# A graph network on one core: edge tiles counted in items of mixed width, and strays gathered by tile

## Chip, cores and metric

One core of one Trainium2 chip. The metric is the device time of one launch in microseconds. A profiled execution of the same kernel gives the trace from which the rows below are read.

## What is computed

6250 nodes with 128 features and 100,000 edges (src, dst), sorted by dst; dst is 6250 u^2 for a uniform u, so the first target nodes have by far the most edges. The layer normalized and rectified x goes through two SAGE convolutions, then through an edge network with batch norm:

```python
def _sage_conv(x, src, dst, W_nbr, W_root, b):
    msgs = x[src]
    summed = jax.ops.segment_sum(msgs, dst, num_segments=N)
    deg = jax.ops.segment_sum(jnp.ones((src.shape[0], 1), x.dtype), dst, num_segments=N)
    agg = summed / jnp.maximum(deg, 1.0)
    return agg @ W_nbr + x @ W_root + b

z = jnp.concatenate([h[src], h[dst], edge_attr], axis=1) @ W.T + b
z = (z - mean) * jax.lax.rsqrt(var + BN_EPS) * gamma + beta
msg = jax.nn.sigmoid(z[:, :H]) * jax.nn.softplus(z[:, H:])
out = x + h + jnp.zeros_like(h).at[src].add(msg)
```

## The kernel before, in words

The nodes are padded to 49 windows of 128 (NT = 49), the edges to 784 tiles of 128, four tiles to a group, 196 groups (NG). The stages follow each other: layer norm, convolution 0, its node products, sort tables, convolution 1, node products and the p and q tables, the edge pass (pass 1, with a gather from p_tab per tile), the message pass (pass 2, with a scatter per tile), the sum of the sorted rows, the output.

**The two convolutions** sum messages x[src] by dst in two ways.

*Counted tiles*: the first 304 tiles (DT), where dst spans few nodes. For a tile, DVE makes two one-hots (`tile_low`: src within its window, 128 wide; `tile_hot`: source window and target slot, up to 392 wide; L1322 to L1331), PE multiplies them (L1667, L1671) into a count matrix of source node by target slot, and ACT copies it to SBUF as bf16 (L918, L922). A unit has eight slots; the first 128 tiles are taken in pairs of two times four slots. Sixteen units are an item, 15 items in all. The item's counts are multiplied with the features of all 49 windows (`final`, L1677, 49 matmuls with 384 columns, the features in three bf16 parts, plus a degree column in convolution 0). The result, 128 target slots by 128 features, goes through ACT and DVE and is added to the sums by window (`sum_acc`, L1697). The counts are stored to DRAM in convolution 0 and loaded again by ACT in convolution 1, so the tiles are built once. An *extra* loop at half way (`conv_extra`) repeats an item's tiles for targets beyond the eighth slot; its least number of rounds is one.

*Gathered groups*: the other 120 groups (76 to 195). POOL gathers the source rows of each tile by indirect DMA (`gather_all`, L826), four to a group, into a ring of eight groups (RP). DVE makes a one-hot of dst against a window (`sum_by_window`, L1221), PE multiplies rows and one-hot (L1687, and the degree column in L1691), DVE adds the sum (L1211). The matmul in L1756 marks a group done, and POOL may then refill its place.

**The order** is written by hand in `conv_slot` of each engine and run by `in_conv`: part 0 has END = 4 slots, part 1 has 7 turns of 2 x CS = 16 slots, part 2 has 4 slots. A slot is one gathered group and a share of the item work (`BUILT`, `FINAL`): in part 0 the first item is built and the features are split into bf16 parts by ACT and DVE in turn (L905, L910, L1338, L1346); in a turn two items are built while the two before them are multiplied. In the first 14 slots of a turn stands one *sort job* each (a histogram by source window in convolution 0, a rank in convolution 1: L1743, L1748, L1749 on PE, L1229, L1236, L1239 on DVE), in every second of these one *root job* (x @ W_root + b for one window: turned by L1727, multiplied by L1731, bias added by L1732, in convolution 1 also x by L1735; copied by ACT, L945). A rank needs a row of `base_tab`, which SP loads when the rank before is done (L689), with x for the root jobs (L697) and the zeroing of rows of m_tab (L669) in the same queue.

POOL waits between groups only for the place in the ring (L821 to L822):

```python
if g >= first + depth:
    pool.wait_ge(freed, before + g - first - depth + 1)
```

## Time and profile before

| | us |
|---|---|
| median of 3 runs | 3615.26 (3613.3 to 3619.41) |
| the profiled execution, own time | 3627.41 |
| its span | 3625.6 |
| busy PE, DVE, ACT, POOL | 2500.5, 1878.3, 1409.1, 2499.9 |
| POOL gathers of the two convolutions (L826 from h_tab) | 956, 958.0 busy |
| mean granted TensorE clock | 0.834 of full |

The profiled execution is one run with its own time; shares and rows are of its span. A busy engine is not yet one that sets the end: what ended an engine's idle time, and whose, says more. The granted clock is 0.5 or 1.0 at any moment (1.2 or 2.4 GHz) and its mean stands in the stage rows.

### The profile page before, as it was taken

The numbers are of one execution on the slowest core, as the hardware profiler recorded it, in microseconds if no ns is written. First come the engines' busy times: TensorE is split into PE (matmuls) and PEld (weight loads), VectorE is DVE, ScalarE is ACT, GpSimd is POOL, SyncE is SP. The second block draws the span as 40 slices with busy tenths as digits, with TensorE's granted clock in tenths as the row PEclk, the third lists the DMA queues.
The fourth block names the chain that finished last, engine by engine and source line by source line (L and its number), as shares of the span: only waits on it lengthen the run. The fifth ranks groups of instructions, "written<-read, shape, count | busy, mean of one in ns | idle before, by whom it ended". The sixth has DMA issues, their size and how long they took to land.

```text
span 3625.6 us, 63849 instructions
## 1 busy us (share of the span) xinstructions
PE 2500.5 (69%) x14630; PEld 1714.2 (47%) x14631; DVE 1878.3 (52%) x4147; ACT 1409.1 (39%) x2642; POOL 2499.9 (69%) x2536
## 2 busy tenths in 40 slices
PE   1888888678888897888888898982222223666348
PEld 0656666545555565544444444441111113656248
DVE  6755655455566665533333333355434335878448
ACT  4333322120100004422222222229878787878600
POOL 5777777477777760777777777765777777777730
PEclk9889988878899998999999999995555556988579
DMA  4444444345455632798888888885544445887358
GB/s 123 150 135 133 133 167 142 121 150 182 155 188 188 203 105 76 256 297 289 290 290 285 288 290 287 290 267 188 175 158 145 159 153 206 292 294 276 113 191 264
DMA packets 337734, 733.52 MB, mean 202 GB/s; under 512 B 66489, under 2 KB 130333, under 8 KB 333761
## 3 DMA queue, kind: packets, MB, share of 16 engines
q1 hardware_dynamic: 242289, 489.81, 38.6%
q0 software_dynamic: 93152, 218.16, 20.1%
q10 hardware_dynamic: 2160, 24.09, 1.7%
q8 instruction: 45, 0.74, 0.1%
q14 instruction: 88, 0.72, 0.1%
HBM read 456.75 MB, written 275.07 MB: 202 GB/s over the span
## 4 chain that ended last, share of the span: by engine, by line
POOL 39%; PE 24%; issue 16%; DMA 6%; DVE 6%; ACT 6%; DVEq 2%; SPq 0%; ACTq 0%; POOLq 0%
POOL m_tab L855 16%; POOL arena L826 8%; POOL H L826 8%; POOL Q L826 7%; PE PS L1687 6%; PE PS L1677 5%; PE PS L1873 3%; DMA m_tab<-Q,pos_i 3%; PE PS L1749 2%; PE PS L1852 1%; PE PS L1857 1%; DMA Q<-base_tab 1%; ACT H L871 1%; DMA H<-p_tab,src_i 1%; PE PS L1843 1%
## 5 line engine op out<-in xcount | busy, mean ns | idle before, releaser
L826 POOL DMA_INDIRECT Q<-h_tab,src_i x956 | 958.0, 1002 | 334.2 <-issue 285.9
L855 POOL DMA_INDIRECT m_tab<-Q,pos_i x782 | 776.5, 993 | 260.2 <-issue 229.2
L1882 PE MATMUL PS<-ident,arena 128*128 128x128 f32 x784 | 193.5, 394 | 621.2 <-DVE arena L1567 377.0
L1687 PE MATMUL PS<-Q 128*128 x2668 | 430.6, 309 | 175.2 <-DVE arena L1211 93.3
L826 POOL DMA_INDIRECT H<-p_tab,src_i x398 | 381.0, 957 | 221.9 <-issue 119.7
L1057 ACT ACTIVATE arena<-PS,LB 128x512 f32<-128x512 f32 x392 | 248.0, 684 | 715.7 <-PE PS L1857 702.2
L1687 PEld LDWEIGHTS PS<-Q 128*128 128x128 f32 x2668 | 366.7, 212 | 260.9 <-issue 257.3
L1882 PEld LDWEIGHTS PS<-ident,arena 128*128 128x128 f32 x784 | 125.8, 197 | 682.8 <-issue 345.1
L826 POOL DMA_INDIRECT arena<-p_tab,src_i x384 | 365.5, 952 | 117.0 <-issue 114.9
L1857 PE MATMUL PS<-arena,WC 128*128 128x512 f32 x784 | 369.4, 593 | 0.0
L1852 PE MATMUL PS<-H,Q 128*128 x1464 | 358.1, 387 | 0.0
L1470 DVE TENSOR_SCALAR H<-arena,wpos 128x512 int16 x244 | 93.5, 383 | 486.0 <-DMA arena<-dst_tab 439.0
L1477 DVE BATCH_NORM_STATS2 stats<-arena 128x512 f32 (+1 forms) x392 | 251.1, 683 | 125.1 <-ACT arena L1057 115.2
L1221 DVE SCALAR_TENSOR_TENSOR Q<-dst_f,wneg,iota 128x512 f32 x322 | 241.8, 751 | 132.0 <-issue 131.9
L1873 PE MATMUL PS<-Q 128*128 128x128 f32 x1872 | 247.3, 295 | 67.1 <-DVE Q L1543 67.1
L1873 PEld LDWEIGHTS PS<-Q 128*128 128x128 f32 x1872 | 239.5, 211 | 72.3 <-DVE Q L1543 70.2
L1852 PEld LDWEIGHTS PS<-H,Q 128*128 x1464 | 145.7, 100 | 135.2 <-issue 18.2
L1857 PEld LDWEIGHTS PS<-arena,WC 128*128 128x128 f32 x784 | 150.3, 192 | 123.5 <-issue 95.6
L1543 DVE TENSOR_TENSOR Q<-Q,PS 128x512 f32<-128x512 f32 x234 | 158.9, 680 | 78.7 <-DMA Q<-m_tab 77.3
L1094 ACT COPY Q<-PS 128x512 f32<-128x512 f32 x196 | 112.0, 571 | 189.1 <-DMA m_tab<-Q,pos_i 179.3
L1559 DVE SCALAR_TENSOR_TENSOR PS<-H,arena 128x512 f32<-128x512 f32 x100 | 69.7, 697 | 218.8 <-ACT arena L1087 218.4
L1211 DVE TENSOR_TENSOR arena<-arena,PS x372 | 105.2, 283 | 139.1 <-PE PS L1691 134.4
(247 smaller groups left out, 4208.8 us busy)
## 6 DMA issues: line engine op xcount, KB each, us to landing
z_tab<-arena SPq DMA_DIRECT2D x196, 512.0 KB
Q<-z_tab SPq DMA_DIRECT2D x196, 512.0 KB, 6.0
Q<-m_tab SPq DMA_DIRECT2D x234, 264.0 KB, 4.7
arena<-in_edge_t SPq DMA_DIRECT2D x196, 256.0 KB, 3.5
m_tab<-arena SPq DMA_DIRECT2D x45, 1056.0 KB
m_tab<-arena SPq DMA_DIRECT2D x14, 2112.0 KB
arena<-dst_tab SPq DMA_DIRECT2D x196, 128.0 KB, 4.3
stats<-m_tab SPq DMA_DIRECT2D x58, 264.0 KB, 6.2
```

The lines of the kernel that those rows point to most:

```text
L826: nc.gpsimd.indirect_dma_start(row(s, k), None, table, bass.IndirectOffsetOnAxis(src_i[:, t:t + 1], 0)).then_inc(landed[s], 16)
L855: nc.gpsimd.indirect_dma_start(m_tab, bass.IndirectOffsetOnAxis(pos_i[:, t:t + 1], 0), mrow[:, s, k, :], None).then_inc(ms.scattered[s], 16)
L1057: ins = nc.scalar.activation(zb[:, s, h * GE:(h + 1) * GE], PS[:, 2 * s + h, :], ACT.Identity, bias=LB[:, h:h + 1])
L1221: v.scalar_tensor_tensor(onehot[:, ds(n % k.banks, 1), 0:n_tiles * P].rearrange("p a (t b) -> p (a t) b", b=P), bc(dst, P), wneg[:, ds(w, 1)],
L1477: ins = v.bn_stats(stats[:, h, ds(g, 1), :].rearrange("p a b -> p (a b)"), zb[:, s, h * GE:h * GE + valid])
L1543: v.tensor_tensor(shot[:, o % SD, :].rearrange("p (a b) -> p a b", b=P), bc(src, P), rep(iota_ps, GT), ALU.is_equal).then_inc(sg.hot_ready, 1)
L1677: return mm(PS[:, 4, 0:cols], item_sums(par)[:, v, :], part_of(v, v + 1)[:, :, 0:cols].rearrange("p a b -> p (a b)"), start=v == 0, stop=v ...
L1687: ins = mm(pair_sums(m % k.banks, slice(0, F)), row(t), oh[:, t * P:(t + 1) * P], start=t == 0, stop=t == n_tiles - 1, skip_group_check=True)
L1852: ins = mm(PS[:, 2 * s + h, :], part, hot, start=False, stop=False, skip_group_check=True)
L1857: ins = mm(PS[:, 2 * s + h, :], WC[:, h * F:(h + 1) * F], ebuf[:, s, :], start=False, stop=True, skip_group_check=True)
L1873: ins = mm(PS[:, SD + o % SD, 0:F], mrow_in[o % MR][:, t, 0:F], shot[:, o % SD, t * P:(t + 1) * P], start=t == 0, stop=t == GT - 1)
L1882: ins = turn(PS[:, 2 + q, t * P:(t + 1) * P], msg_t[:, q, t * P:(t + 1) * P], ident[:])
```

## The change

The counted tiles grow from 304 to 352, the gathered groups fall from 120 to 108 in each convolution. The items are no longer alike: `SPECS` gives tiles in a unit, slots of a unit and units, `ORDER` the order in which items are built (14, 64, 14, 42, 14, 32, 14, 30, 16, 16, 18, 18, 18, 21, 21 tiles). A pair now shares one block of slots and is summed in PSUM, with one eviction for the unit. A one-hot tile is as wide as its unit's slots times 49, with the slot as the outer index. A turn has 14 slots (CS = 7), the ends have five (END = 5), the ring of rows has seven groups (CR) in the convolutions, the ring of tiles ten (HR). `FINAL` gives eight or nine windows to a slot. The extra rounds go; a target beyond its unit's slots (a stray) is handled by a loop over tiles at the middle of the convolution (`MIDDLE`): POOL gathers the rows of one tile again and DVE and PE add those whose dst is marked in `wide_dst`. It runs one round if no tile has a stray, otherwise 352. The sort jobs fill all 14 slots. The bias of a root job is a product with three bf16 rows; in convolution 1 DVE adds x (`add_root`). On SP the order within a pair of sort jobs changes, and DVE computes the windows of the items and the mask of strays inside the first slots of part 1.

```diff
-    IT = P // SPAN
-    ITEMS, FINE = 15, 4
-    UNITS = ITEMS * IT
-    FT = 2 * FINE * IT
-    DT = UNITS + FINE * IT
-    WIDE = DT // IT
-    HALF_SPAN = SPAN // 2
-    HH = NT * HALF_SPAN
+    SPECS = ([(2, 4, 32), (2, 6, 21), (2, 8, 16), (2, 8, 15)] + [(1, 6, 21)] * 2 + [(1, 7, 18)] * 3
+             + [(1, 8, 16)] * 2 + [(1, 9, 14)] * 4)
+    ORDER = [14, 0, 13, 1, 12, 2, 11, 3, 10, 9, 8, 7, 6, 5, 4]
+    FROM = [sum(n * units for n, _, units in SPECS[:i]) for i in range(len(SPECS) + 1)]
+    ITEM = [(FROM[i],) + SPECS[i] for i in ORDER]
+    ITEMS, DT, SPAN = len(ITEM), FROM[-1], 9
+    PAIRED = sum(n * units for n, _, units in SPECS if n == 2)
+    UNIT_AT = [sum(units for _, _, _, units in ITEM[:m]) for m in range(ITEMS + 1)]
+    TILE_AT = [sum(n * units for _, n, _, units in ITEM[:m]) for m in range(ITEMS + 1)]
+    LEAST = min(slots * units for _, slots, units in SPECS)
     DG = DT // GT
     DP = DT // (2 * GT)
-    HW = NT * SPAN
-    HR = 8
-    CS, END = 8, 4
-    RP = 8
+    HW = (SPAN + 1) * NT
+    HOT = 448
+    HR = 10
+    CS, END = 7, 5
+    RP, CR = 8, 7
     OD, LATE = 8, 3
     CD = [2, 4]
     CITER = ITEMS + 1
     PAIRS = (CITER - 2) // 2
-    HALFWAY = FINE // 2
-    SO_FAR = 2 * HALFWAY + 1
-    BUILT = {END: [0, 4, 8, 12, IT], CS: [0, 2, 4, 6, 8, 10, 12, 14, IT]}
-    FINAL = {END: [0, 17, 34, NT, NT], CS: [0, 7, 14, 21, 28, 35, 42, NT, NT]}
...
-        rows, a = carve(q_space, a, RP * GT, F)
+
+        rows, a = carve(q_space, a, CR * GT, F)
         tile_stats, _ = carve(q_space, a, NT, 6)
...
+        def tiles_in_slot(m, u, n_slots):
+
+            n = TILE_AT[m + 1] - TILE_AT[m]
+            return range(n * u // n_slots, n * (u + 1) // n_slots)
+
+        def unit_of(m, t):
+
+            _, n, slots, _ = ITEM[m]
+            return t // n, t % n == 0, t % n == n - 1, slots
...
-            for to, tab in ((slot_dst, slot_tab), (wide_dst, wide_tab)):
-                sp.dma_start(to, tab.rearrange("(m p) -> p m", p=P), allow_slow_non_contiguous=True).then_inc(tiles_in, 16)
+            for m, (t0, n, slots, units) in enumerate(ITEM):
+                sp.dma_start(slot_tab[m * P:m * P + units * slots].rearrange("(u k) -> u k", k=slots),
+                             tile_slot_tab[t0:t0 + units * n, 0:slots].rearrange("(u n) k -> u n k", n=n)[:, 0, :]
+                             ).then_inc(natural_stored, 16)
+            sp.wait_ge(natural_stored, 96 + 16 * ITEMS)
+            sp.dma_start(slot_dst, slot_tab.rearrange("(m p) -> p m", p=P), allow_slow_non_contiguous=True).then_inc(natural_stored, 16)
 
             def zero_rows(g, n):
...
-                    load_x(i + 1)
                     sp.wait_ge(srt.ranked, i * 2 + 2)
                     load_base(i * 2 + 2)
+                    sp.wait_ge(root.done, i + 2 + NT)
+                    load_x(i + 1)
                     if i1 == ZN:
                         zero_rows(i * ZG + 2 * PAIRS * Z1, ZG)
...
                 depth = len(landed)
                 for g in range(first, NG):
+                    if table is not p_tab and g == MIDDLE:
+                        pool.wait_ge(wide.ready, 1)
+                        with pool.Fori(0, wide_rounds(pool)) as x:
+                            pool.wait_ge(wide.used, tick(pool, wides))
+                            nc.gpsimd.tensor_copy(wide_col, src_i[:, ds(x, 1)]).then_inc(wide.copied, 1)
+                            pool.wait_ge(wide.copied, pool.snap(wides, min_val=1, max_val=2 * DT))
+                            pool.sem_inc(wait_done, 1)
+                            nc.gpsimd.indirect_dma_start(wide_row, None, table,
+                                                         bass.IndirectOffsetOnAxis(wide_col, 0)
+                                                         ).then_inc(wide.landed, 16)
...
+                def evict_unit(m, par, i):
+                    slots = ITEM[m][2]
+                    return nc.scalar.copy(item_sums(par)[:, :, i * slots:(i + 1) * slots],
+                                          PS[:, 2 + (UNIT_AT[m] + i) % 2, 0:slots * NT].rearrange("p (k v) -> p v k", v=NT))
...
+                        evict_unit(m, parity(part, s), i).then_inc(dn.evicted, 1)
                     jr = root_job(part, s, b)
                     if jr is not None:
                         act.wait_ge(root.turned, jr + (1 + c * NT))
                         nc.scalar.copy(hst, PS[:, 5, 0:F]).then_inc(root.lhs, 1)
+                    jr = root_job(part, s - 1, b)
+                    if jr is not None and c == 0:
+                        act.wait_ge(root.product, jr + 1)
+                        nc.scalar.copy(H[:, jr, :], PS[:, 5, F:2 * F]).then_inc(root.done, 1)
...
+
+            def item_tables():
+
+                for m, (t0, n, _, units) in enumerate(ITEM):
+                    groups = slice(t0 // GT, (t0 + n * units - 1) // GT + 1)
+                    v.tensor_reduce(item_lo[0:1, m:m + 1], word_lo[0:1, groups], AX.X, ALU.min)
+                    ins = v.tensor_reduce(item_hi[0:1, m:m + 1], word_hi[0:1, groups], AX.X, ALU.max)
+                step(ins)
+                step(v.scalar_tensor_tensor(words3[0:1, :], item_lo[0:1, :], 64.0, item_hi[0:1, :], ALU.mult, ALU.add))
+
+            def wide_tables():
+
+                step(v.tensor_tensor(wide_dst, dst_f[:, 0:DT], wide_dst, ALU.subtract))
+                for i, (_, slots, _) in enumerate(SPECS):
+                    t = slice(FROM[i], FROM[i + 1])
+                    v.tensor_scalar(span_row[0:1, t], span_row[0:1, t], float(slots), None, ALU.is_ge)
+                    ins = v.tensor_scalar(wide_dst[:, t], wide_dst[:, t], float(slots), None, ALU.is_ge)
+                step(ins)
+                step(v.scalar_tensor_tensor(wide_dst, dst_f[:, 0:DT], 1.0, wide_dst, ALU.add, ALU.mult))
+                step(v.tensor_scalar(wide_dst, wide_dst, -1.0, None, ALU.add))
+                step(v.tensor_reduce(span_row[0:1, DT:DT + 1], span_row[0:1, 0:DT], AX.X, ALU.max))
+                step(v.tensor_scalar(span_row[0:1, DT:DT + 1], span_row[0:1, DT:DT + 1], float(DT), 1.0, ALU.mult, ALU.max))
+                v.tensor_copy(rounds[:], span_row[0:1, DT:DT + 1]).then_inc(wide.ready, 1)
+                dve.wait_ge(wide.ready, 1)
...
+                def hot_tile(m, t):
+
+                    t0, n, slots, _ = ITEM[m]
+                    col, r, width = t0 + t, (TILE_AT[m] + t) % HR, (slots * NT + 1) // 2 * 2
+                    v.tensor_scalar(tile_low[:, r, :], low_iota, src_low[:, col:col + 1], None, ALU.is_equal)
+                    return v.tensor_scalar(tile_hot[:, r, 0:width], hot_iota[:, 0:width], src_key[:, col:col + 1], None, ALU.is_equal)
```

On DVE's slot, its x for the root, and on PE:

```diff
-                            for t in range(built[x % CS], built[x % CS + 1]):
-                                d = tile_of(n, t)
-                                dve.wait_ge(dn.built, n * IT + t + 1)
-                                (hot_pair(t, d) if n < FINE else hot_tile(t, d, src_key[:, d:d + 1])
-                                 ).then_inc(dn.hot_ready, 1)
+                            for t in tiles_in_slot(n, x % CS, slots_of(part)):
+                                dve.wait_ge(dn.built, TILE_AT[n] + t + 1)
+                                hot_tile(n, t).then_inc(dn.hot_ready, 1)
...
                         place_by_rank(js, s % 2)
+                    jr = root_job(part, s - 1, b)
+                    if jr is not None and c == 1:
+                        add_root(jr)
+                    if c == 0 and (part, s, b) == (1, 0, 0):
+                        item_tables()
+                    if c == 0 and (part, s, b) == (1, 2, 0):
+                        wide_tables()
                     if part > 0 and u == slots_of(part) - 2:
+                        if c == 0 and m == 1:
+                            dve.wait_ge(natural_stored, 112 + 16 * ITEMS)
                         dve.wait_ge(dn.acc_taken, m + c * ITEMS)
...
+                    with dve.Fori(0, wide_rounds(dve)) as x:
+                        g = dve.snap(x // GT, min_val=0, max_val=DG - 1)
+                        sum_by_window(k, g, words, pair, before, wide_dst[:, ds(x, 1)], 1)
...
+                def add_root(jr):
+
+                    dve.wait_ge(root.product, jr + (1 + NT))
+                    dve.wait_ge(x_in, jr * 16 + 16)
+                    v.tensor_tensor(H[:, ds(jr, 1), :].rearrange("p a f -> p (a f)"), PS[:, 5, F:2 * F], xs, ALU.add
+                                    ).then_inc(root.done, 1)
...
+                    dve.wait_ge(in_w, 160)
+                    for c2, B in enumerate((B1, B2)):
+                        high, mid, low = (bias_parts[:, c2, j, :] for j in range(3))
+                        step(v.tensor_copy(high, B[:]))
+                        step(v.tensor_tensor(B[:], B[:], high, ALU.subtract))
+                        step(v.tensor_copy(mid, B[:]))
+                        step(v.tensor_tensor(low, B[:], mid, ALU.subtract))
+                        step(v.tensor_scalar(high, high, ident[:, 0:1], None, ALU.mult))
+                        step(v.scalar_tensor_tensor(high, mid, ident[:, 1:2], high, ALU.mult, ALU.add))
+                        v.scalar_tensor_tensor(high, low, ident[:, 2:3], high, ALU.mult, ALU.add).then_inc(consts, 1)
...
+                def build(m, t):
+                    i, first, last, slots = unit_of(m, t)
+                    r = (TILE_AT[m] + t) % HR
+                    if first:
+                        pe.wait_ge(dn.evicted, UNIT_AT[m] + i + 1)
+                    return mm(PS[:, 2 + (UNIT_AT[m] + i) % 2, 0:slots * NT], tile_low[:, r, :], tile_hot[:, r, 0:slots * NT],
+                              start=first, stop=last)
...
-                            pe.wait_ge(x_in, jr * 16 + 16)
-                            ins = mm(PS[:, 5, F:2 * F], ident[:], xs, start=False, stop=True)
-                        ins.then_inc(root.product, 1)
+                        mm(PS[:, 5, F:2 * F], ones_bf[0:3, :], bias_parts[0:3, c, 0, :], start=False, stop=True
+                           ).then_inc(root.product, 1)
...
+                def wide_tiles():
+
+                    with pe.Fori(0, wide_rounds(pe)) as x:
+                        landed_now = pe.snap(tick(pe, wides) * 16)
+                        lo, hi = windows(pe, pe.snap(x // GT, min_val=0, max_val=DG - 1))
+                        pe.wait_ge(wide.landed, landed_now)
+                        with pe.Fori(lo, hi):
+                            sum_rows(lambda t: wide_row, 1, ones_bf[:, 0:1])
+                        mm(PS[:, 7, 0:1], ones_bf[:], ones_bf[:, 0:1], start=True, stop=True).then_inc(wide.used, 1)
+
```

## Rows read from the trace of the kernel before

**Rows 1.** busy by stage: length, PE, PEld, DVE, ACT, POOL, clock, DMA share, GB/s
```profile
41.00:677.00 636.00, 502.34 (x4165) 378.75 (x4166) 372.18 (x1167) 194.49 (x548) 486.36 (x478) 0.89 0.41 136
...
721.00:1345.00 624.00, 526.52 (x2814) 348.97 (x2814) 373.10 (x831) 65.20 (x195) 471.58 (x478) 0.87 0.52 170
```

**Rows 2.** groups of POOL, 41 to 690 and 715 to 1345; busy, mean | idle before
```profile
L826 POOL DMA_INDIRECT Q<-h_tab,src_i x478 | 486.5, 1018 | 180.3 <-issue 146.6 <-DMA h_tab<-H 31.0 <-PE PS L1756 2.7
...
L826 POOL DMA_INDIRECT Q<-h_tab,src_i x478 | 471.6, 987 | 153.8 <-issue 139.3 <-PE PS L1756 12.2 <-DMA h_tab<-H 2.4
```

**Rows 3.** line L826 by itself, same two stretches: min/median/max ns, first and last start
```profile
L826 POOL DMA_INDIRECT Q<-h_tab,src_i x478: 940/944/2621, 41.3 to 676.2; - x160
...
L826 POOL DMA_INDIRECT Q<-h_tab,src_i x478: 940/944/2088, 721.2 to 1343.3; - x160
```

**Rows 4.** timeline of POOL at its two pauses
```profile
105.22 0.94 POOL L826 DMA_INDIRECT Q<-h_tab,src_i  x1 [4.28 <-issue]
...
957.72 0.94 POOL L826 DMA_INDIRECT Q<-h_tab,src_i  x1 [6.39 <-PE PS L1756]
```

**Rows 5.** waits of PE, 41 to 691: total us, times, longest
```profile
PE PS L1687 <- DMA Q<-h_tab,src_i: 21.6, 9, 7.3
```

**Rows 6.** waits of PE, 721 to 1366
```profile
PE PS L1748 <- DMA Q<-base_tab: 20.7, 7, 3.8
...
PE PS L1687 <- DMA Q<-h_tab,src_i: 0.7, 1, 0.7
```

**Rows 7.** timeline of PE, line L1756: it marks the end of a gathered group
```profile
103.89 0.16 PE L1756 MATMUL PS<-ones_bf 128*128 128x1 bf16 x1
...
690.20 0.17 PE L1756 MATMUL PS<-ones_bf 128*128 128x1 bf16 x1 [0.27 <-issue]
...
922.82 0.17 PE L1756 MATMUL PS<-ones_bf 128*128 128x1 bf16 x1
...
956.70 0.21 PE L1756 MATMUL PS<-ones_bf 128*128 128x1 bf16 x1
...
1277.35 0.21 PE L1756 MATMUL PS<-ones_bf 128*128 128x1 bf16 x1
...
1364.40 0.17 PE L1756 MATMUL PS<-ones_bf 128*128 128x1 bf16 x1
```

**Rows 8.** timeline of DVE: the start, and one slot with four narrow tiles
```profile
54.07 0.47 DVE L1294 TENSOR_TENSOR Q<-dst_f,arena 128x304 f32<-128x304 f32 x1 [4.15 <-DMA Q<-wide_tab]
...
106.68 0.74 DVE L1221 SCALAR_TENSOR_TENSOR Q<-dst_f,wneg,iota 128x512 f32 x1
...
107.54 0.24 DVE L1322 TENSOR_SCALAR arena<-Q 128x128 bf16<-128x128 int16 x1
...
107.88 0.24 DVE L1322 TENSOR_SCALAR arena<-Q 128x128 bf16<-128x128 int16 x1
...
109.39 0.74 DVE L1221 SCALAR_TENSOR_TENSOR Q<-dst_f,wneg,iota 128x512 f32 x1
```

**Rows 9.** groups over the span: the wide tiles' one-hots
```profile
L1331 DVE TENSOR_SCALAR Q<-Q 128x392 bf16<-128x392 int16 x208 | 69.8, 336 | 0.0
```

**Rows 10.** timeline of PE over two slots of the second convolution
```profile
970.46 0.17 PE L1756 MATMUL PS<-ones_bf 128*128 128x1 bf16 x1
...
972.85 1.16 PE L1687 MATMUL PS<-Q 128*128 x8
973.84 0.17 PE L1756 MATMUL PS<-ones_bf 128*128 128x1 bf16 x1
...
975.33 0.48 PE L1732 MATMUL PS<-B,ones 1*128 1x128 f32 x2
...
976.06 0.33 PE L1748 MATMUL PS<-Q,upper_bf 128*128 128x392 bf16 x1
```

**Rows 11.** DMA issues, 724 to 1343: KB each
```profile
arena<-count_tab ACTq DMA_DIRECT2D x7, 1568.0 KB
```

**Rows 12.** chain that ended last, 530 to 540: start, us, what
```profile
532.53 2.42 DMA Q<-h_tab,src_i
```

265 lines of the change are left out of this document (77 added, 188 removed).

## The prediction

> **What bounds the kernel now.** I read the busy time by stage first [rows 1]. The two convolutions take 636 and 624 us of 3625.6; the edge pass (1445 to 2429) and the message pass behind it issue nothing of what the change touches, so the time has to come from the first 1366 us. In both convolutions POOL looks no busier than 77%, but the group behind that share [rows 2] is a gather of about 1.0 us followed by 0.30 us of "issue" in which it waits for nobody: POOL issues gathers back to back, 1.018 + 0.30 = 1.32 us each in the first convolution and 0.987 + 0.30 = 1.29 in the second. 478 of them are 630 and 615 us, which is the distance between the first and the last gather start, 635 and 622 [rows 3], less its only two real pauses: 4.28 us before 105 and 6.39 us before 958 [rows 4]. So POOL sets both lengths.
>
> Who is next is the second question, and the two convolutions differ. In the first, PE waits for gathered rows nine times, 21.6 us [rows 5]: it is ahead and starved. In the second it waits for them once, 0.7 us [rows 6]. There PE trails POOL by most of the ring: its extra round at half way takes it from 922.82 to 956.70, and from there to 1277.35 it does 64 groups, 80.2 us for a turn of 16 [rows 7], hardly less than POOL's 64 x 1.29 = 82.4. POOL is the bound there too, but PE is only 2 us a turn quicker.
>
> **Part by part.** *Fewer gathers.* The counted tiles go from 304 to 352, so the gathered groups from 120 to 108 in each convolution: 48 gathers less, 48 x 1.32 = 63.3 us in the first and 48 x 1.29 = 61.8 in the second, on POOL's path.
>
> *The stray gather.* POOL now stops once at the middle of each convolution for one count load, one small copy, a wait for it and one gather. The gather is 1.3 us; the load, copy and wait are in no row for POOL. Lower end 1.5 us in all (the copy at nothing), upper end 8 (the longest pause POOL has, 6.4, and a gather). I take 3.5 for each, near the lower end, since the round waits for no other engine in its first turn. With no stray the loop runs once: the inputs of the reference, tile by tile, give largest spans of 3, 5, 6 and 7 for units of 4, 6, 8 and 8 slots in the paired items, and 4 to 8 for 6 to 9 slots in the others, so no edge lies outside its unit.
>
> *The start of the first convolution.* The first four groups are paced by the splits and end at 103.89 [rows 7], which is the 4.28 us pause. The ring is one group shorter now, so group k+7 waits for group k. On the other side the slow strided load of wide_tab goes out of DVE's start (its landing ended DVE's wait at 54 [rows 8]), and the first item has 14 tiles in five slots. I keep these even. Then comes the item with 64 tiles in seven slots, 9.1 a slot, where before it was 4. DVE makes one narrow tile in 0.34 us (107.54 to 107.88 [rows 8]) and its other work in such a slot is 109.39 - 106.68 - 4 x 0.34 = 1.35 us. But the ring of tiles is 10 deep: it can prepare only one or two tiles of the next slot before PE has built those of this one, and PE builds them only after the last group's sum. That makes a chain in series: one-hot 0.74, PE's sum and ones 1.5, eight tiles 2.8, the sort's one-hot 0.55, together 5.6 us, 5.9 with the second windows, where POOL needs 4 x 1.32 = 5.3. Seven slots lose 4 us; the item tables (30 small reductions) and the stray tables (some 36 operations) stand in DVE's order in the same slots, 3 and 5 us, and nothing covers them while the ring is empty. With the old pause that is 4 + 8 + 3 or 4 = 15 us of pause in place of 4.3. Ends: 0, and 30 if PE's half clock falls on it. Later items have 6 tiles a slot or less and are hidden: PE's catching up there is what [rows 5] shows.
> A rule speaks against this part too. What the rows show: the gather's median is 944 ns in the first convolution, with DVE's 640 tile operations beside it (two for each of 128 narrow and 192 wide tiles), and 944 in the second, with the other 16 of the 208 wide tiles [rows 3, 9]; only the means differ, by 31 ns. The Trainium skill (SBUF — State Buffer, section SBUF: two separate sides) says that a VectorE tensor_scalar in a 2-port mode holds the port pair, so that GpSimd can't write descriptors until it ends. By that page the gathers would wait through the hot tiles; the sum above goes without it, by the equal medians.
> First convolution: -63.3 + 3.5 + 11 = -49 us.
>
> *Turns of seven groups in the second.* Here PE decides. All times in this part are from PE's rows [rows 6, 7, 10]. Its extra round goes: 33.9 us for a slot that otherwise takes 5, -29. In a turn two group sums go (972.85 to 973.84 is 1.0 us for one window, 1.34 windows, and 1.15 for the clock that PE gets: -3.1). The root's bias and x products go from PE, 975.33 to 976.06 [rows 10], with one short product in their place: 0.65 x 7 x 1.15 = -5.2; x is added by DVE, 0.29 us, beside it. The 14 sorts and 98 window products are only packed closer. Closer packing has a price: a base row that is late costs PE 3.0 us, seven times [rows 6], once a turn, when the item's counts, 1568 KB [rows 11], load beside it. The slots behind the turn's second load had no sort until now; all 14 have one after, so I add one such wait: +3.0. A turn is 80.2 - 3.1 - 5.2 + 3.0 = 74.9 us, above POOL's 56 x 1.29 = 72.2. Seven turns: -37. The two ends have five slots for four: +6.8 (two of 3.4, as 970.46 to 973.84 [rows 10]). The stray round +3.5. Sum: -29 - 37 + 6.8 + 3.5 = -56 us. Ends: -72 if POOL stays bound (-61.8 - 6.4 + 3.5, and PE's tail behind the last gather falls from 21 us to the first convolution's 14 [rows 3, 7]), -35 if the turns give only a third of their 37 us.
>
> *Costed at nothing.* Wider tiles and 352 builds for 320 on DVE and PE in the first convolution: hidden behind POOL by the slack that [rows 5] shows; without that cover they are 5 us a turn. Evictions by unit (268 for 256) on ACT, which is 31% busy [rows 1]. 15 small slot copies and the slot load on SP's queue: first needed at the second item's end. The three-part bias on DVE, 14 small operations before the first split, 3 us: given back by the earlier load. SP's later order of the x load: the zeroing of rows goes behind it by a slot and is waited for far later.
>
> **Sum.** -49 - 56 = -105 us against the profiled execution, 3627.4 (span 3625.6 and 1.8 around it): 3522. The runs' median is 3615.3, 12 below it, so **3510**.
>
> **Rivals.**
> *POOL stays the bound in both.* For: its pauses are 10.7 us in two convolutions, and my extra wait for base rows is argued from when loads fall. Against: PE's 80.2 us a turn. It gives -49 - 72: 3494.
> *The 64-tile item costs twice as much.* If build, eviction and tile wait on each other with two banks, the slot is 8 to 9 us, a pause of 37 in place of 15: 3531. Against: at 108 to 131 four tiles a slot cost PE nothing visible.
> *Descriptors blocked by hot tiles.* All of the dense item's 64 x 0.34 = 22 us would be added to POOL: 3531. The medians speak against it. This is what the page SBUF — State Buffer of the Trainium skill would make of the item.
> *Strays, slower.* One edge beyond its unit's slots makes the count 352 rounds in each convolution, not one, in series on POOL, DMA and PE: 1.3 for the gather, 2.4 for its landing [rows 12], 1.3 for sum and one-hot, 5 us. 704 x 5 = +3500 us, some 7000 in all. It decides from the first such edge. Before, the 208 wide tiles in the trace are the items' 176 and one round of 16 in each convolution, which shows no span of 8 or more, but not that the units of 4 to 7 suffice; for that I have the inputs alone.
>
> **How the numbers follow.** Forecast 0.60; POOL bound 0.20; dense item 0.09; blocked descriptors 0.04; strays 0.02; no net gain or something unseen 0.05, of which 0.025 faster all the same, 0.015 without a change and 0.01 slower. The range takes both rivals near 3531 and the ends of the unknown costs: -64 - 72 = -136 below, and -35 for the first (a pause of 30 in place of 15) and -35 above: 3479 to 3545. A measurement of this kernel tells about 0.2%, 7 us. Faster by more than that 0.955, within it 0.015, slower 0.03.
>
> **What would show it.** Right: 430 gathers a convolution at a median of 944 ns; one pause or several of about 15 us in all between 100 and 160; in the second convolution PE at some 75 us a turn, base rows waited for some 14 times, POOL pausing a few us in each turn; no block of 49 window products in a row at half way. If POOL bounds both, its pauses in the second vanish and PE waits for rows there. If the dense item is worse, groups end 8 us apart from 110 on. If gathers lengthen while tiles are made, it is the ports. Wrong altogether: more than one stray gather, or a rest behind 1445 that doesn't keep its 2180 us.

## The result, and the profile after

The changed kernel takes 3567.0 us in the median (3561.9 to 3568.6, 4 runs) against 3615.4: 48 us faster, a ratio of 0.9861 with a 95% interval of 0.9843 to 0.988. Forecast were 3510 us and 105 less; 3567 lies above the range of 3479 to 3545. Half of the gain is missing. The profiled execution took 3567.8 (span 3565.9), 59.7 less in span than the profiled one of before, which was itself 12 above its median.

The two convolutions by stage, first to last gather, as in [rows 1]:

```profile
41.00:635.00 594.00, 471.29 (x3911) 353.84 (x3912) 381.59 (x1270) 192.69 (x558) 438.32 (x432) 0.88 0.42 140
679.00:1279.00 600.00, 484.19 (x2476) 316.86 (x2477) 362.95 (x814) 44.83 (x129) 426.34 (x432) 0.81 0.52 172
```

The first fell from 636 us to 594, 7 short of the 49 forecast. The second fell from 624 only to 600, although POOL is busy for 45 us less in it. The granted clock in it fell from 0.87 to 0.81.

POOL's groups, first in 41 to 650, then in 679 to 1279 (busy, mean | idle before), which answer to [rows 2]:

```profile
L848 POOL DMA_INDIRECT Q<-h_tab,src_i x430 | 437.6, 1018 | 185.8 <-issue 123.4 <-PE PS L1754 31.4 <-DMA h_tab<-H 31.0
...
L848 POOL DMA_INDIRECT Q<-h_tab,src_i x430 | 425.2, 989 | 174.8 <-issue 122.9 <-PE PS L1754 49.5 <-DMA h_tab<-H 2.4
```

430 gathers at the same means as before, 1018 and 989 ns, and the same 0.3 us of issue. New is the wait for PE: 31.4 and 49.5 us, where [rows 2] had 2.7 and 12.2. A gather waits there for a free place in the ring of gathered rows, so PE was late in both.

The same gather line alone, 41 to 640 (min/median/max ns, first and last start), and POOL's timeline at its first pause, its longest, its last in that run of pauses, and at the stray round; these answer to [rows 3, 4]:

```profile
L848 POOL DMA_INDIRECT Q<-h_tab,src_i x430: 938/944/2088, 41.1 to 634.5; - x144
```
```profile
92.82 0.94 POOL L848 DMA_INDIRECT Q<-h_tab,src_i  x1 [3.11 <-PE PS L1754]
...
137.50 0.94 POOL L848 DMA_INDIRECT Q<-h_tab,src_i  x1 [5.49 <-PE PS L1754]
...
166.24 1.26 POOL L848 DMA_INDIRECT Q<-h_tab,src_i  x1 [3.48 <-PE PS L1754]
...
239.46 0.94 POOL L848 DMA_INDIRECT Q<-h_tab,src_i  x1 [0.30 <-issue]
240.41 0.20 POOL L833 COPY Q<-src_i 128x1 int32 x1
241.39 0.97 POOL L836 DMA_INDIRECT Q<-h_tab,Q  x1 [0.79 <-POOL Q L833]
242.67 1.06 POOL L848 DMA_INDIRECT Q<-h_tab,src_i  x1 [0.30 <-issue]
```

In the first convolution there are ten pauses over 0.6 us, 29.2 us in all: two of 3.1 in the end slots, seven of 1.2 to 5.5 between 113 and 166, and the stray round, which is one gather and costs 2.0 us in all (242.67 against 240.70, where the next gather would have begun). In the second the pauses sum to 47.9 us: the stray round at 853, and all the others between 931 and the end.

PE's waits in the second convolution, 679 to 1305 (total us, times, longest), for [rows 6]:

```profile
PE PS L1746 <- DMA Q<-base_tab: 65.3, 26, 8.6
PE PS L1687 <- DVE Q L1219: 22.2, 22, 3.8
PE PS L1687 <- DVE arena L1209: 21.3, 22, 9.6
```

This is the line that counts. PE waits 65.3 us for base rows, 26 times, where it waited 20.7 us, 7 times. It is the price that the prediction knew, on a larger scale. Seven turns of 14 groups end at these marks (PE's timeline, line L1754, [rows 7]):

```profile
715.42 0.21 PE L1754 MATMUL PS<-ones_bf 128*128 128x1 bf16 x1
...
1281.56 0.17 PE L1754 MATMUL PS<-ones_bf 128*128 128x1 bf16 x1
```

566.1 us for seven turns are 80.9 each: a turn of 14 groups now takes what a turn of 16 took (80.2 in the prediction), where 74.9 was forecast.

The waits have places. Counted by the job's position in its turn: the 7th waits in every turn, 16.8 us together; the last, the 14th, in six of seven, 39.1 us; the others share 9. One of the long ones, on the three queues. First SP's, with the issue times of x, of a zeroing of four groups (1056 KB), and of the base row:

```profile
863.52 0.36 SPq L706 DMA_DIRECT2D Q<-in_x  x1
864.09 0.42 SPq L678 DMA_DIRECT2D m_tab<-arena  x1
865.25 0.24 SPq L698 DMA_DIRECT2D Q<-base_tab  x1
```

Then ACT's, the item's count table of 1568 KB:

```profile
864.17 0.35 ACTq L944 DMA_DIRECT2D arena<-count_tab  x1
```

And PE's, which waits for the base row and then goes on:

```profile
867.80 0.22 PE L1733 MATMUL PS<-bias_parts,ones_bf 3*128 3x128 bf16 x1
874.69 0.50 PE L1746 MATMUL PS<-Q,upper_bf 128*128 128x392 bf16 x1 [6.67 <-DMA Q<-base_tab]
875.12 1.67 PE L1747 MATMUL PS<-Q,ones 1*128 1x392 f32 x2
```

The 1.5 KB base row is issued at 865.25 and used at 874.69, 9.4 us later, with a megabyte ahead of it on its own queue and a megabyte and a half beside it. Elsewhere in the turn, with no large transfer beside it, such a row is used 2.2 us after its issue. What follows the wait matters too: L1747's pair takes 1.67 us here, at a granted clock of half, and 0.92 in a slot without a wait (864.15 in the same turn), at the full one.

The rest keeps its length: from the last group to the end it is 2261.8 us, 2261.0 before.

### The profile page after: what moved, and what is told of

It reads as the page before. It is cut to its first block, busy times and chain, and to the rows that moved or that the text cites. A ratio compares the mean times of both kernels' runs of the same rounds, so it can differ in the third digit from the quotient of the medians.

```text
span 3565.9 us, 61360 instructions
## 1 busy us (share of the span) xinstructions
PE 2419.9 (68%) x13970; PEld 1656.5 (46%) x14064; DVE 1881.8 (53%) x4242; ACT 1386.9 (39%) x2586; POOL 2408.7 (68%) x2444
## 4 chain that ended last, share of the span: by engine, by line
POOL 36%; PE 29%; issue 15%; DMA 7%; DVE 6%; ACT 4%; DVEq 2%; SPq 0%; POOLq 0%; ACTq 0%
POOL m_tab L877 18%; POOL arena L848 9%; POOL H L848 8%; PE PS L1687 8%; PE PS L1677 7%; DMA Q<-base_tab 3%; PE PS L1861 3%; PE PS L1747 2%; DMA m_tab<-Q,pos_i 2%; PE PS L1672 1%; PE PS L1845 1%; PE PS L1840 1%; ACT H L893 1%; POOL Q L848 1%; DVEq L1217 1%
## 5 line engine op out<-in xcount | busy, mean ns | idle before, releaser
L848 POOL DMA_INDIRECT Q<-h_tab,src_i x860 | 862.7, 1003 | 360.6 <-issue 246.3
L1687 PE MATMUL PS<-Q 128*128 x2456 | 409.2, 315 | 142.8 <-DVE arena L1209 76.8
L1687 PEld LDWEIGHTS PS<-Q 128*128 128x128 f32 x2456 | 347.5, 217 | 227.7 <-issue 224.7
L1840 PE MATMUL PS<-H,Q 128*128 x1371 | 337.2, 384 | 5.4 <-issue 0.7
L1861 PEld LDWEIGHTS PS<-Q 128*128 128x128 f32 x1872 | 242.3, 213 | 71.9 <-DVE Q L1548 69.6
L1219 DVE SCALAR_TENSOR_TENSOR Q<-dst_f,wneg,iota 128x512 f32 x294 | 221.2, 752 | 93.3 <-issue 92.8
L974 ACT COPY Q<-PS 128x128 f32<-128x128 f32 x98 | 26.2, 267 | 515.2 <-PE PS L1728 487.9
```

Of the source, the lines that this page charges most:

```text
L848: nc.gpsimd.indirect_dma_start(row(s, k), None, table, bass.IndirectOffsetOnAxis(src_i[:, t:t + 1], 0)).then_inc(landed[s], 16)
L1219: v.scalar_tensor_tensor(onehot[:, ds(n % k.banks, 1), 0:n_tiles * P].rearrange("p a (t b) -> p (a t) b", b=P), bc(dst, P), wneg[:, ds(w, 1)],
L1687: ins = mm(pair_sums(m % k.banks, slice(0, F)), row(t), oh[:, t * P:(t + 1) * P], start=t == 0, stop=t == n_tiles - 1, skip_group_check=True)
L1840: ins = mm(PS[:, 2 * s + h, :], part, hot, start=False, stop=False, skip_group_check=True)
L1861: ins = mm(PS[:, SD + o % SD, 0:F], mrow_in[o % MR][:, t, 0:F], shot[:, o % SD, t * P:(t + 1) * P], start=t == 0, stop=t == GT - 1)
```

## The experiments

The ratios are to the kernel before, timed on the same chip beside them. Beside the change, and in two of the six later sets of runs, it took 3614 to 3627 us at a mean granted clock near 0.835; in four sets it took 4327 to 4377 us at 0.77. These two conditions are compared only within themselves, and the second is told at the end. All times are medians.

**Order and latency of the small load.** First the SP queue's order: the zeroing goes ahead of the wait for the root's end, and not behind it.

```diff
+                    if i1 == ZN:
+                        zero_rows(i * ZG + 2 * PAIRS * Z1, ZG)
                     sp.wait_ge(root.done, i + 2 + NT)
                     load_x(i + 1)
-                    if i1 == ZN:
-                        zero_rows(i * ZG + 2 * PAIRS * Z1, ZG)
```

> The changed kernel, with one move on SP in the second convolution: the zeroing of 1056 KB goes out before the wait for the root sum and the load of x, not behind them, so the base row that follows is issued some 3 us behind it, not 1.0 to 1.4. Theory (base rows late behind the zeroing and the counts hold PE): waits for base rows fall from 64.6 us to about 38, the ones at the fourteenth job of a turn from 6.5 us each to 3.5, the second convolution 25 to 32 us shorter, total near 3540. Rival (a turn of 14 is held by PE's and DVE's own work, the waits only show it): other waits of PE take their place, under 8 us gained, 3560 or more.

Measured: 3568.8 us, 0.9868 (0.985 to 0.9886), no faster than the change. Yet the base-row waits did fall, by 19 us:

```profile
PE PS L1746 <- DMA Q<-base_tab: 45.9, 13, 5.1
PE PS L1687 <- DVE arena L1209: 34.8, 38, 9.6
PE PS L1687 <- DVE Q L1219: 25.6, 26, 3.8
```

The small waits went and the 14th position fell to 20.2 us, but the 7th rose to 25.7, and the waits for DVE rose by 17 us, it seems because PE arrived sooner at things that were not ready. The second convolution was 11 us shorter in this profile (613.9 from its first gather to its last group's end, 624.9 in the changed kernel), but that profile is of the fastest of the five runs (3556.6), and the median doesn't show it. The expectation missed (45.9 us of waits where 38 were expected, and 3569 us where 3540 were); its rival, 3560 us or more with other waits in their place, is what came.

Next, the base row loses its place in series: two buffers for it, so that each is loaded two ranks ahead.

```diff
-        brow, a = carve(q_space, a, WT * NT)
+        brow, a = carve(q_space, a, 2, WT * NT)
...
-                    load_base(i * 2 + 1)
+                    load_base(i * 2 + 2, 0)
...
-                    load_base(i * 2 + 2)
+                    load_base(i * 2 + 3, 1)
```

> The changed kernel with two buffers for the base row and a semaphore each, so a row is asked for one job earlier. Theory: no wait of PE for base rows above 1 us in all, a turn falls from 80.7 us to the 72 of POOL's 56 gathers, PE at full clock more of the time, the second convolution 45 to 55 us shorter, total near 3518. Rival (own work of PE and DVE): a turn stays above 77 us, under 25 us gained, 3542 or more.

Measured: 3512.7 us (3508.8 to 3519.0), 0.9717 (0.9699 to 0.9734): 54 us less than the changed kernel. That lies 3 us from the number of the prediction, by luck, as is told below. PE's waits, and the marks of the seven turns:

```profile
PE PS L1686 <- DVE arena L1208: 35.3, 40, 9.6
PE PS L1686 <- DVE Q L1218: 25.3, 26, 3.8
PE PS L1644 <- DVE Q L1251: 12.0, 1, 12.0
PE PS L1686 <- DMA Q<-h_tab,src_i: 11.5, 3, 5.9
```
```profile
716.84 0.17 PE L1753 MATMUL PS<-ones_bf 128*128 128x1 bf16 x1
...
1231.04 0.17 PE L1753 MATMUL PS<-ones_bf 128*128 128x1 bf16 x1
```

No base row is waited for. A turn takes 514.2 / 7 = 73.5 us, near POOL's 72.2. POOL pauses for 2.3 us, at the stray round alone (47.9 before the edit), and PE waits for gathered rows: POOL is the bound again, as the theory said. One buffer more gives back the whole missing half, so the late base rows are its cause.

**Which transfer delays it.** With one buffer again, each of the two large transfers was taken away, and then both. The zeroing:

```diff
                     zero_rows(b * (2 * Z1) + h * Z1, Z1)
+                    zero_rows(2 * PAIRS * Z1 + (2 * b + h) * 12, 12)
+            zero_rows(2 * PAIRS * Z1 + 2 * PAIRS * 12, ZN * ZG - 2 * PAIRS * 12)
...
-                    if i1 == ZN:
-                        zero_rows(i * ZG + 2 * PAIRS * Z1, ZG)
```

and the counts, of which three quarters are left out in the second convolution: this kernel multiplies stale counts there and computes a wrong result, so its time serves for this comparison alone:

```diff
-    act.dma_start(item_sums(par).rearrange("p v t -> p (v t)"), square(count_tab, m)
+    act.dma_start(item_sums(par).rearrange("p v t -> p (v t)")[:, 0:NT * P // 4], square(count_tab, m)[:, 0:NT * P // 4]
```

The first runs of these fell in a set at the lower clock; they were repeated with the changed kernel beside them.

> The 45 zeroings of the second convolution's aggregate groups (1056 KB each) are all issued in the first convolution, where the base rows are not used. Theory (the base row of 1.5 KB, fetched in series with the ranks, lands late behind the zeroing): the waits for base rows at the last position of each turn, 39 us in the changed kernel, go, and the small ones (8 us) with them; the 17 to 25 us at the seventh position stay, since there the load of a dense count table is under way beside it. Waits 65 to about 20 to 25 us, the stretch of the second convolution's turns 20 to 30 us shorter. The first convolution may give back up to 5 us for the zeroing it takes on. About 3548 us. Rival (the waits are the plain latency of a base row and the zeroing is beside the point): waits over 50 us, 3560 to 3570 us.

> The second convolution loads a quarter of each dense count table (about 0.4 MB in place of 1.5 MB) and leaves out the rest, so its dense products work on old counts, with the same instructions in the same order; the zeroing stays. Theory (two large transfers delay the base row, each at its own position in the turn): the waits at the seventh position, 17 us, go; those at the last position stay at 25 to 39 us, since the zeroing is still just ahead of the base row. Waits 65 to about 45 us; about 3555 us. If the last position's waits fall under 15 us, it was the two together and neither alone. Rival (the waits are plain latency): nothing changes, 3567 us.

> Both edits together: all zeroing in the first convolution and a quarter of each count table in the second; one buffer for the base row, as in the changed kernel. This measures what the series of rank, base row and next rank costs by itself. Theory (a base row alone takes 2.2 to 3.4 us from issue to use, which fits between two rank products 5.3 us apart): no more than 5 us of base-row waits are left, and the time is that of the kernel with two base-row buffers, 3512 us, within 10 us. Rival (a fetch in series with the ranks is itself too slow at this pace): over 20 us of waits are left and the time is 3530 us or more.

> The changed kernel itself, unedited, as the yardstick of the three kernels timed with it: four earlier runs of edited kernels were on a chip where the kernel before took 4334 us and TensorE's granted clock was lower. Where the kernel before takes about 3615 us again, this one takes 3560 to 3570 us with 60 to 65 us of base-row waits; where it takes about 4330 us, TensorE sets the pace in both convolutions and this one takes 4140 to 4160 us.

> As the first run of this edit: all zeroing in the first convolution. Theory at a kernel before of about 3615 us: base-row waits 65 to 20 to 25 us, those at the seventh position alone; 3548 us, about 15 to 20 us under the changed kernel timed beside it. Rival (plain latency): no difference. At a kernel before of about 4330 us: the waits are partly covered, and it is within 10 us of the changed kernel.

> As the first run of this edit: a quarter of each dense count table is loaded in the second convolution, the rest is left out. Theory at a kernel before of about 3615 us: the waits at the seventh position go, those at the last stay at 25 to 39 us; about 10 us under the changed kernel. Rival: no difference.

> As the first run of this edit: both together, one base-row buffer. Theory: under 5 us of base-row waits and a time within 10 us of the kernel with two base-row buffers (3512.7 us where the kernel before takes 3614 us), that is about 50 us under the changed kernel. Rival (a fetch in series with the ranks is itself too slow): over 20 us of waits left, and at most 35 us under the changed kernel.

Measured in the repetition (the kernel before 3626.8 us): the changed kernel 3568.4, ratio 0.9837 (0.9821 to 0.9854); zeroing moved 3549.0, 0.9794; counts at a quarter 3534.8, 0.9745; both 3521.4, 0.9712 (0.9695 to 0.9728). The base-row line of PE's waits for the four, in this order, one fence for each kernel:

```profile
L1746 PE MATMUL PS<-Q,upper_bf 128*128 128x392 bf16 x98 | 36.0, 368 | 66.3 <-DMA Q<-base_tab 66.3
```
```profile
PE PS L1746 <- DMA Q<-base_tab: 40.9, 13, 4.8
```
```profile
PE PS L1746 <- DMA Q<-base_tab: 26.7, 20, 3.9
```
```profile
L1746 PE MATMUL PS<-Q,upper_bf 128*128 128x392 bf16 x98 | 34.5, 352 | 4.3 <-DMA Q<-base_tab 4.2
```

| | 7th position, us | 14th | others | second convolution | end of the first | time against the changed kernel |
|---|---|---|---|---|---|---|
| changed | 18.1 | 39.1 | 9 | 627.9 | 650.9 | |
| zeroing moved | 20.2 | 20.7 | 0 | 581.7 | 662.2 | -19 |
| counts at a quarter | 0.5 | 16.6 | 9.5 | 596.6 | 650.8 | -34 |
| both | 0.5 | 3.7 | 0 | 563.9 | 664.6 | -47 |

The second convolution is read from its first gather to its last group's end, in the one profile of each kernel; the time is by medians. Moving the zeroing isn't free: the first convolution's last group ends 11 to 14 us later for it. So the column of times understates the zeroing. In the second convolution alone it is worth 46 us, and the counts 31.

So both theories of the runs hold in part. At the 7th position it is the count table alone. At the 14th it is both: 39.1 falls to 20.7 without the one, to 16.6 without the other, to 3.7 without either. The small waits are the zeroing's. My expectation for the moved zeroing said that the 14th would go; it halved, and the 3549 us, 1 from what was expected, came with twice the waits expected and a price in the first convolution: luck. The one for the counts said that the 14th would stay at 25 us or more; it fell to 16.6. With both away the series of rank, load and rank still stands and costs 4 us, as expected: the single buffer alone is harmless, what hurts is a load in series that lands behind large ones.

**The first convolution.** Two edits, alone and with the two buffers. One moves the item of 64 tiles from second to sixth place (the items around it shift with it), the other computes the mask of strays (`wide_tables`, which some of the expectations call the sorting tables) six slots later:

```diff
-    ORDER = [14, 0, 13, 1, 12, 2, 11, 3, 10, 9, 8, 7, 6, 5, 4]
+    ORDER = [14, 10, 13, 1, 12, 0, 11, 2, 9, 3, 8, 7, 6, 5, 4]
...
-                    if c == 0 and (part, s, b) == (1, 2, 0):
+                    if c == 0 and (part, s, b) == (1, 8, 0):
```

> The changed kernel with the item of 64 tiles built sixth, not second (order 14, 10, 13, 1, 12, 0, 11, 2, 9, 3, 8, 7, 6, 5, 4), so that the ring of rows is full when it comes. Theory of the dense chain: of the 29 us in which POOL pauses in the first convolution, those between 113 and 166 (20.7 us) fall to 8 or less and none of more than 4 us appears at the later place, total 10 to 16 us below 3567. Rival (the ends of seven groups and the table work make the pauses whatever the item): pauses between 105 and 170 stay above 15 us, total within 5 us of 3567.

> The changed kernel with the mask of strays (wide_tables, on DVE) computed in the ninth slot of part 1, not the third. Theory (it stands in DVE's order while the ring is empty, 5 us): POOL's pauses of the first convolution fall from 29 to 23 to 25 us, total 3560 to 3564. Rival (DVE has room there, the dense chain hides it): within 2 us of 3567.

> A version meant to be the fastest: two buffers for the base row, the dense items in an order that puts the first two-tile item as the sixth in place of the second, and the sorting tables built six slots later. With base-row waits gone in the second convolution (3512.7 us measured with two buffers alone) the two edits act on the first convolution alone, where GpSimd pauses 29 us. Theory (those pauses are set by the early two-tile items and the tables): the first convolution is 5 to 10 us shorter than with two buffers alone, 3503 to 3508 us. Rival (each pause only moves to another place, as in the two kernels that tried one edit alone): within 4 us of 3512 us.

Measured: the item moved 3566.0 us, 0.9868; the tables moved 3564.3, 0.9864; neither differs from the change by what a measurement tells (7 us). With the item moved, POOL's timeline has nothing between the end slots and 225; then it pauses here:

```profile
101.14 0.94 POOL L848 DMA_INDIRECT Q<-h_tab,src_i  x1 [3.11 <-PE PS L1754]
...
280.27 0.94 POOL L848 DMA_INDIRECT Q<-h_tab,src_i  x1 [1.87 <-PE PS L1754]
...
288.68 1.03 POOL L848 DMA_INDIRECT Q<-h_tab,src_i  x1 [3.17 <-PE PS L1754]
...
311.43 0.94 POOL L848 DMA_INDIRECT Q<-h_tab,src_i  x1 [5.10 <-PE PS L1754]
```

The pauses go with the item: 21.6 us in all in place of 29.2. The last gather starts 4.0 us sooner, but PE's tail behind it is longer and the last group ends at 653.6 in place of 650.1. So most of these pauses belong to the item of 64 tiles, as its theory said, but at the new place there is one of 5.1 us, which it ruled out, and moving the item gains nothing. With the tables moved the pauses sum to 27.2 us and the last group ends 2.8 us sooner (647.3), less than a measurement of the whole kernel tells.

Both edits with two base-row buffers ran four times, three beside the two buffers alone, always at the lower clock. At the ordinary one the combination wasn't timed.

> The kernel with two base-row buffers once more, as the yardstick of the run beside it. Where the kernel before takes 3614 to 3627 us: 3513 to 3523 us, no base-row wait. Where it takes over 4300 us, TensorE's clock sets the pace: about 4140 us.

> The version meant to be the fastest once more: two base-row buffers, the second of the two-tile items moved from second to sixth place and the sorting tables built six slots later. Theory (the early pauses of GpSimd come from these two): pauses in the first convolution 30 to about 15 to 20 us and 5 to 10 us under the kernel beside it. Rival (a pause only moves, since the work that TensorE has to do in the first convolution stays the same): within 4 us of it.

> Two base-row buffers, the yardstick of the run beside it. Where the kernel before takes 3614 to 3627 us: 3513 to 3523 us. Where it takes over 4300 us: 4140 to 4180 us.

> Two base-row buffers, the second two-tile item in sixth place and the tables six slots later. Theory (the first convolution's pauses come from these two edits' places): pauses there 30 to 15 to 20 us, and 5 to 10 us under the kernel beside it. Rival (a pause only moves): within 4 us of it, with the sum of the pauses near 25 us. Where the kernel before takes over 4300 us: within 4 us, as before.

> Two base-row buffers, the yardstick of the run beside it: 3513 to 3523 us where the kernel before takes 3614 to 3627 us, 4160 to 4180 us where it takes over 4300 us.

> Two base-row buffers, the second two-tile item in sixth place, the tables six slots later. Theory (the first convolution's pauses come from the places of these two): pauses there 30 to 15 to 20 us, 5 to 10 us under the kernel beside it. Rival (a pause only moves): pauses near 25 us, within 4 us of it. Where the kernel before takes over 4300 us: no difference.

Measured (two buffers; all three edits): 4177.5 and 4174.6 us; 4173.9 and 4183.8; 4137.5 and 4131.7: -3, +10 and -6 us. No gain: the runs of a single kernel spread by 7 to 23 us here. In these sets the first convolution isn't bound as it was. POOL's group there, 41 to 800, with two buffers alone (a wait "remote" is one for which the profile names no engine):

```profile
L847 POOL DMA_INDIRECT Q<-h_tab,src_i x430 | 435.0, 1012 | 337.0 <-PE PS L1753 128.8 <-issue 110.5 <-remote 66.9
```

POOL waits 129 us for PE, and the stage ends at 811 us instead of 650. Its gathers are as fast as ever (1012 ns), so it isn't POOL that is slow. The stage with two buffers, at the ordinary clock and at the lower one:

```profile
41.00:650.00 609.00, 483.42 (x4025) 363.80 (x4026) 386.48 (x1284) 192.82 (x560) 437.60 (x432) 0.89 0.42 137
```
```profile
41.00:811.00 770.00, 542.77 (x4028) 396.18 (x4028) 388.70 (x1284) 186.38 (x560) 436.06 (x432) 0.83 0.33 109
```

PE's busy time grows by 59 us where the stage grows by 161, so the granted clock explains only a part. The rest is idle time, and a part of it follows PE's products. DVE's add into the sums (L1208) starts 0.32 us after the end that the profile shows for PE's sum at the ordinary clock (median of the 56 adds for which DVE had stood idle over 0.6 us, at most 0.45), and 1.3 us at the lower one (of 62, up to 4.6). The other way round nothing is later: PE starts as soon behind DVE as before. Whether PE's products really end later than the profile draws them, or its signals travel late, isn't shown. Here the two buffers give 0.9553, 0.953 and 0.9572, 190 to 203 us, and the four edited kernels of the first such set, in the order zeroing, counts, both, all three: 4147.3, 4133.5, 4131.4 and 4133.9 us (0.9559, 0.9525, 0.953, 0.9523). The first of them, which at the ordinary clock is 28 us behind the third, is 16 us behind it here. The gain of the change by itself wasn't measured at this clock, and the kernel before has no profile there, so where its larger gain comes from isn't shown.

## Why the prediction was half right

The second convolution is told first, from its first gather's start to its last group's end: 643.4 us before, 624.9 after. -18.5 measured, -56 forecast.

*The step that failed* is the added wait, "so I add one such wait: +3.0", and under it the sentence that costed SP's later order "at nothing", because "the zeroing of rows goes behind it by a slot and is waited for far later". Nobody waits for the zeroing, that is true. But it is queued ahead of a small load that is waited for. Before, each zeroing was issued 0.45 us behind a base row, and the next row followed it by 3.0 us or more; now it waits with x for the root's end, and in half of the cases goes out 1.0 to 1.4 us ahead of a base row. SP's timeline of before, to lay beside the three issues above:

```profile
847.77 0.36 SPq L697 DMA_DIRECT2D Q<-in_x  x1
849.68 0.23 SPq L689 DMA_DIRECT2D Q<-base_tab  x1
850.13 0.42 SPq L669 DMA_DIRECT2D m_tab<-arena  x1
```

And the two slots without a sort, which the prediction named, were the cover of the second count load. I saw this and took the price of the one row that showed a wait, 3.0 us, which is a base row beside a count table. The new position has a count table and, as long as there are rows to zero, a zeroing, and no row had that pair; a wait there cost 6.5 us in the mean, 6.4 to 8.6 in the four turns with the zeroing just ahead and 4.3 in the one that has none left. Forecast were 20.7 + 21 = 42 us of such waits, measured 65.3: 24 of the 37 missing.

*The clock* is the second part, and it is shown less well. The 2601 products of PE between these marks have 504.3 us of busy time in the changed kernel and 488.2 with two buffers: 16 us more for the same instructions, at a mean clock of 0.81 against 0.85.

```profile
679.00:1304.00 625.00, 504.26 (x2601) 331.42 (x2601) 374.42 (x842) 45.10 (x130) 426.34 (x432) 0.81 0.50 165
```
```profile
681.00:1253.00 572.00, 488.15 (x2598) 323.02 (x2599) 372.35 (x839) 45.06 (x130) 430.36 (x432) 0.85 0.55 181
```

The timeline shows where. The longest wait, and the first slot behind it against one at the full clock:

```profile
1107.30 0.92 PE L1747 MATMUL PS<-Q,ones 1*128 1x392 f32 x2
1108.15 2.05 PE L1687 MATMUL PS<-Q 128*128 x16
...
1122.83 0.50 PE L1746 MATMUL PS<-Q,upper_bf 128*128 128x392 bf16 x1 [8.59 <-DMA Q<-base_tab]
1123.27 1.67 PE L1747 MATMUL PS<-Q,ones 1*128 1x392 f32 x2
1124.87 3.78 PE L1687 MATMUL PS<-Q 128*128 x16
```

0.75 + 1.73 us lost in these two groups alone. The rank product behind every one of the 11 waits of 2.8 us or more ran at half clock; of all 196 products of L1747 it was 32, against 12 with two buffers. So a long wait is paid here once as idle time and again in the work behind it.

How much of the 16 us this is isn't settled. The clock also falls without such a wait: 19 times in this stage, and still 17 times with two buffers. And the 16 us are the difference of two single profiles. The changed kernel's second profile has 509 us of busy time for these products, and the two kernels whose edits are made for the first convolution (told above) have 496 (item moved) and 502 (mask moved); their base-row waits are 66, 63 and 59 us. With the zeroing moved it is 489 at 40.9 us of waits, with the counts at a quarter 507 at 26.7. So the busy time doesn't follow the sum of the waits, and that the base rows cost all of these 16 us isn't shown.

24 + 16 = 40 us, against 37.5 missing: the sizes fit, but the second rests on single profiles, which lie up to 13 us apart at nearly the same waits. The other terms so roughly hold together, not each by itself. Held: the root's bias and x, forecast -5.2 a turn, -36.6: the groups that went were 24.2 + 24.0 us, the one that came

```profile
L1733 PE MATMUL PS<-bias_parts,ones_bf 3*128 3x128 bf16 x49 | 11.3, 230 | 0.0
```

-36.9. The block at half way is gone with its 33.9 us slot. Too large was the saving on group sums, forecast -22 us: L1687's busy time went only from 215.1 to 210.2. Unforeseen was a gain beside it: PE's waits for DVE fell from 72.1 us to 43.5, part of it with the extra round.

*With the wait away* the sum for the second convolution is right: 74.9 less the 6.0 us of base-row waits that it held is 68.9 a turn, under POOL's 72.2, so POOL would bound; the two-buffer kernel measured 73.5, and 572.8 us for the stage, -70.6 where the rival "POOL stays the bound" said -72. That the whole came to 3512.7, beside the 3510 forecast for another kernel, is luck. For a kernel without this wait the prediction's terms give -49 - 72, its rival's 3494. Against that the start of the second convolution came 8 us less early, 40.6 for 49, the rest behind it took 2.8 more, and the profile of before lay 12 us above its median where this one lay 6 above its own.

*The first convolution.* -49 forecast, -41.7 measured by the last gather (676.2 to 634.5), -40.3 by the last group. The 48 gathers fell as reckoned, 63.3 us. The stray round took 2.0 us, not 3.5. The pauses were taken as 15 us and are 26.9 without the stray's: 6.2 in the end slots for 4.3 before, which I had kept even, and 20.7 for the item and the tables, taken as 12. That lies half way to the rival of the double item, 37. -63.3 + 22.6 more of pause - 2.4 (the 0.30 that each of eight new pauses contains) + 2.0 = -41, which closes. The stray tables were right in size (DVE works on them from 124.85 to 129.83, 5.0 us), and the kernel that moves them doesn't tell whether it costs anything.

*Other rivals.* Descriptors blocked by hot tiles: none. The mean gather is 1018 ns in both kernels, with 704 tile operations beside them in place of 640, and the median 944. Gather by gather in the changed kernel: the 185 that overlap such an operation take 1029 ns in the mean, the other 245 take 1009; before, it was 1010 for 172 and 1022 for 306. The Trainium skill (SBUF — State Buffer, section SBUF: two separate sides) would have these gathers wait while a tensor_scalar of VectorE in a 2-port mode holds the ports; the trace doesn't agree. Strays: one round in each convolution, as the inputs said, and the rest behind the convolutions kept its length.

*The chances.* Faster by over 0.2% was right. The range was too narrow above: it allowed the turns to give a third of their 37 us, and they gave none. The list of what would show it named the right row, base rows waited for some 14 times; it was 26.

## What to carry to other kernels

A large transfer that nobody waits for is not free: cost it by the small load behind it on its queue, and the one beside it, wherever an engine waits for that. When slots that did nothing are packed away, list what used to land in them; here two idle slots covered a load, and closing them made it land 9 us after its issue and not 2. A load in series with compute wants a second buffer, of 3 KB in all here, before anything around it is made denser.

## What the runs showed of the hardware that was not expected

The latency of one 1.5 KB row, from issue to use, was 2.2 us with its queue free, near 5 us with 1568 KB under way from another queue, and 9.3 to 10.0 with 1056 KB issued 1.0 to 1.4 us ahead on its own as well. With the 1056 KB ahead alone it was 3.2 to 3.9. So the two together delay it by more than the sum of each alone. And the same kernels took 20% longer in sets in which the mean granted clock was 0.77 and not 0.835: 4327 to 4377 us against 3614 to 3627 for the kernel before, with unchanged gathers on POOL. In the first convolution PE's busy time accounts for 59 of the 161 us more, and what waits for PE goes on later behind the end that the profile shows. The change's gain with two buffers was 4.3 to 4.7% there and 2.8% here, so a ratio holds for the condition in which it was taken.
